# Gate and up of the second layer's experts: from float32 matmuls to three float32r products of split operands

## The chip, the cores and the metric

The kernel runs on one core of a Trainium2 chip. The metric is device time in microseconds (us), lower is better. TensorE (PE) multiplies, with its weight loads shown apart as PEld; VectorE (DVE), ScalarE (ACT) and GpSimd (POOL) work on vectors; SyncE (SP) issues most DMAs. A name with a q behind it (PEq, PEldq, DVEq) is that engine's sequencer, which reads the instruction stream, computes addresses and waits for semaphores.

## What is computed

Two layers, each cross attention and then a mixture of experts, on a sequence of 2048 tokens of width 256. The change lies in the second layer's mixture. Cut from the reference:

```python
x = hidden_states.reshape(-1, d)                 # 2048 x 256
scores = jax.nn.sigmoid(x @ W_gate_router)       # 8 experts
_, sel = jax.lax.top_k(scores + expert_bias, 2)
shared = jax.nn.silu(x @ Wg_s) * (x @ Wu_s) @ Wd_s
xr = x[tok]                                      # every token twice
h = jax.nn.silu(jnp.einsum('nd,edf->enf', xr, Wg)) * jnp.einsum('nd,edf->enf', xr, Wu)   # f = 192
out_all = jnp.einsum('enf,efd->end', h, Wd)
routed = out_all[exp, jnp.arange(exp.shape[0])] * w
out = shared.at[tok].add(routed)
```

Gate and up are the two products with Wg and Wu. Both are taken at once: 256 inputs against 2 x 192 = 384 columns.

## The kernel before, in words

The second mixture has three parts in a row, each a block that all engines leave together.

`route_and_share` computes the router, the shared branch and the place of each token in a list sorted by expert. POOL scatters the normalised tokens to that list in DRAM with 32 indirect DMAs (L1355) and at the end waits until they have landed. Meanwhile SP loads the weights of all 8 experts into SBUF (`resident["up"]` and `resident["down"]`, in the trace `keep_f_up` and `keep_f_down`), and waits for them (`resident_in`). PE, ACT and DVE compute the shared branch; its float32 products for gate and up are already made of three float32r products: a `high` part (ACT, L1410 and L1416), a `low` part, original minus `high` (DVE, L1459 and L1466), and then high x high, high x low and low x high (PE, L1389).

`run_resident_slots` works through 39 slots of 128 sorted tokens, one expert each. The order of each engine is that of the code, in a software pipeline: step s does the gate and up of slot s, the turning (transposing) of the rows of slot s + 1, the turning of the hidden values of slot s - 1 and the down product of slot s - 2. The steps 3 to 36 are a hardware loop, two steps in a pass; the others stand out straight. Within a step:

- POOL: `send(s - 5)` issues an indirect DMA of a finished slot's result (L1906), `stage_rows(s)` copies the rows of a slot (L1891).
- PE: two register loads of the expert's number from SBUF (L1934, `value_load`), which PE's sequencer turns into addresses; `go_up(s)` (L1950), `turn_rows(s + 1)` (L1941), `turn_hidden(s - 1)` (L1960), `go_down(s - 2)` (L1969). Waits stand in `wait` (L71, and L73 where it puts a nop behind the wait, `apart=True`).
- ACT: the activation of gate (L2003), then the copy of turned rows to SBUF, `x_t` (L1995).
- DVE: the product of gate and up (L2017), the copy of the turned hidden values (L2022), the copy of the result (L2026).

A float32 matmul of the program shows as two MATMUL records in the trace, so `go_up`, 2 matmuls of 384 columns, shows as 4.

`collect` then loads the results back and adds them up.

## Time and profile before

| | us |
|---|---|
| median of 3 runs (lowest, highest) | 1779.78 (1776.4, 1784.43) |
| the profiled execution, its time | 1767.28 |
| its span, first to last instruction | 1765.5 |
| PE busy | 1484.7 (84%) |
| DVE busy | 1160.5 (66%) |
| ACT busy | 856.5 (49%) |
| mean granted clock of PE | 0.914 of full speed |

The share of busy time is a mean over stages with different limits. The attention and the first layer fill the span up to about 1500 us; the change concerns what lies behind, 1522 us (start of the router) to 1743 us (start of `collect`). PE's granted clock is given as a share of 2.4 GHz: 1.00 is 2.4 GHz, 0.50 is 1.2 GHz. The PE durations of single matmuls include the time from first column to last result; how fast a row of them goes is read from the distance of their starts.

### The profile page before, as it was taken

How to read it: one execution, taken by the hardware profiler on the slowest of the kernel's cores; microseconds unless marked ns; L12 is line 12 of the kernel's file. 1: busy time of each engine (PE TensorE's matmuls, PEld its weight loads, DVE VectorE, ACT ScalarE, POOL GpSimd, SP SyncE). 2: the span in 40 equal slices, each digit the busy share in tenths (PEclk: the TensorE clock that was granted, in tenths of full speed). 3: DMA queues.
4: the chain of work that ended last, by engine and by line, in shares of the span. 5: the costliest groups of instructions: out<-in, count | busy, mean ns of one | idle time of the engine just before them, and what ended most of it. 6: DMA issues, size and time to landing. Idle time of an engine off the chain costs nothing. (4 is left out here: it accounts for less than half of the span.)

```text
span 1765.5 us, 23798 instructions
## 1 busy us (share of the span) xinstructions
PE 1484.7 (84%) x7833; PEld 870.6 (49%) x7834; DVE 1160.5 (66%) x2277; ACT 856.5 (49%) x1537; POOL 237.3 (13%) x357
## 2 busy tenths in 40 slices
PE   5769889779996999994499999999999999675883
PEld 3333333367885788883253333433443434553551
DVE  5739889464112677775399999999999973531334
ACT  3214777522212555551317777777777786231110
POOL 2000000001202333331000000000000000064443
PEclk9787999878998999997659999999999999697997
DMA  8844121120103899982533211111121100525114
GB/s 287 349 143 136 44 56 46 42 92 13 38 1 129 292 341 341 332 314 81 153 87 89 46 25 42 30 24 24 32 40 24 24 2 1 119 78 164 39 42 164
DMA packets 107534, 190.84 MB, mean 108 GB/s; under 512 B 10702, under 2 KB 80323, under 8 KB 107431
## 3 DMA queue, kind: packets, MB, share of 16 engines
q1 hardware_dynamic: 97521, 159.31, 28.7%
q0 software_dynamic: 7584, 27.93, 4.3%
q10 hardware_dynamic: 2326, 2.31, 0.4%
q8 instruction: 55, 0.90, 0.2%
q14 instruction: 48, 0.39, 0.1%
HBM read 145.20 MB, written 43.79 MB: 107 GB/s over the span
## 5 line engine op out<-in xcount | busy, mean ns | idle before, releaser
L1099 DVE TENSOR_REDUCE attend_piece_max<-attend_p_bank 128x1 f32<-128x400 f32 (+3 forms) x1280 | 669.5, 589 | 66.5 <-PE attend_p_bank L982 54.3
L1079 ACT ACTIVATE attend_probs<-attend_s_bank 128x512 f32<-128x512 f32 (+1 forms) x1053 | 549.6, 606 | 232.4 <-PE attend_s_bank L996 232.1
L982 PE MATMUL attend_p_bank<-attend_k_st,attend_q_st 62*128 62x400 f32 (+2 forms) x1280 | 416.0, 435 | 41.6 <-DMA attend_q_st<-q_rows 19.4
L996 PE MATMUL attend_s_bank<-attend_q_st,attend_k_st 64*128 64x512 f32 (+1 forms) x1053 | 390.3, 447 | 39.4 <-ACT attend_probs L1079 13.2
L996 PEld LDWEIGHTS attend_s_bank<-attend_q_st,attend_k_st 64*128 64x128 f32 (+1 forms) x1053 | 168.3, 184 | 347.3 <-ACT attend_probs L1079 326.0
L1013 PE MATMUL attend_o_bank<-attend_probs,attend_v_st 128*32 128x512 f32 (+1 forms) x2176 | 291.0, 607 | 2.2 <-ACT attend_probs L1079 2.1
L982 PEld LDWEIGHTS attend_p_bank<-attend_k_st,attend_q_st 62*128 62x128 f32 x1280 | 208.6, 195 | 89.4 <-issue 39.1
L1753 DVE TENSOR_TENSOR slots_w_low<-slots_w_up,slots_w_high 128x2048 fp32r<-128x2048 f32 x46 | 110.4, 2402 | 45.7 <-ACT slots_w_high L1749 45.7
L1540 DVE TENSOR_TENSOR share_hid<-share_b_bank,share_g_act 128x512 f32<-128x512 f32 (+1 forms) x40 | 27.6, 691 | 116.5 <-PE share_b_bank L1389 105.4
L957 POOL COPY attend_v_st<-attend_values 128x64 f32<-128x64 f32 (+1 forms) x32 | 9.2, 296 | 692.2 <-PE attend_o_bank L1013 658.3
L1749 ACT ACTIVATE slots_w_high<-slots_w_up 128x2048 fp32r<-128x2048 f32 x46 | 87.7, 1908 | 5.9 <-DMA slots_w_up<-in_L_ffn_W_dram 5.7
L1709 PE MATMUL slots_y_bank<-slots_w_dn,slots_hid_t 128*128 128x256 f32 x368 | 83.2, 379 | 1.0 <-DVE slots_hid_t L1760 1.0
L1662 POOL DMA_INDIRECT back<-slots_y_sb,slots_target x23 | 61.6, 2677 | 152.9 <-DVE slots_y_sb L1809 152.9
L2017 DVE TENSOR_TENSOR slots_hid<-slots_u_bank,slots_g_act 128x192 f32<-128x192 f32 x39 | 14.0, 358 | 101.2 <-ACT slots_g_act L2003 101.2
L1401 PE MATMUL share_y_bank<-share_w_dn,share_hid 128*128 128x256 f32 (+1 forms) x320 | 71.3, 382 | 5.9 <-DVE share_hid L1540 5.9
L1709 PEld LDWEIGHTS slots_y_bank<-slots_w_dn,slots_hid_t 128*128 128x128 f32 x368 | 69.9, 190 | 11.4 <-issue 1.2
L1013 PEld LDWEIGHTS attend_o_bank<-attend_probs,attend_v_st 128*32 128x32 f32 (+1 forms) x2176 | 43.0, 108 | 64.7 <-ACT attend_probs L1079 32.0
L1950 PE MATMUL slots_u_bank<-keep_f_up,slots_x_t 128*128 x156 | 62.0, 521 | 14.4 <-issue 11.9
L1401 PEld LDWEIGHTS share_y_bank<-share_w_dn,share_hid 128*128 128x128 f32 (+1 forms) x320 | 59.6, 190 | 17.5 <-DVE share_hid L1540 8.9
L1426 ACT ACTIVATE share_g_act<-share_a_bank 128x512 f32<-128x512 f32 (+1 forms) x40 | 23.9, 598 | 79.5 <-PE share_a_bank L1389 79.5
L1773 ACT ACTIVATE slots_g_act<-slots_a_bank 128x512 f32<-128x512 f32 x46 | 27.2, 592 | 71.3 <-PE slots_a_bank L1687 71.3
L1355 POOL DMA_INDIRECT sorted<-keep_x_x_n,keep_f_place x48 | 48.7, 1014 | 96.2 <-DVE keep_f_place L1523 82.3
(264 smaller groups left out, 1844.2 us busy)
## 6 DMA issues: line engine op xcount, KB each, us to landing
slots_w_up<-in_L_ffn_W_dram SPq DMA_DIRECT2D x46, 1024.0 KB, 7.2
slots_w_dn<-in_L_ffn_W_dram SPq DMA_DIRECT2D x23, 1024.0 KB, 5.6
prep_raw<-in_mask_BxSxS_ik_dram POOLq DMA_DIRECT2D x16, 800.5 KB, 8.4
attend_q_st<-q_rows SPq DMA_DIRECT2D x64, 128.0 KB, 3.1
sorted<-keep_zeros SPq DMA_DIRECT2D x6, 1088.0 KB, 7.8
k_rows<-prep_k_part SPq DMA_DIRECT2D x8, 800.5 KB, 6.0
attend_k_st<-k_rows SPq DMA_DIRECT2D x32, 200.1 KB, 3.6
collect_back<-back SPq DMA_DIRECT2D x12, 512.0 KB, 7.0
```

The costliest lines, as they stand in the source:

```text
L982: last = pe.matmul(bank[:, 0:even(kn)], q_st[rows, slot, t * P:(t + 1) * P].bitcast(F32R), k_st[rows, slot, k0:k0 + even(kn)].bitcast(F32R ...
L996: last = pe.matmul(out, k_st[rows, hs, kt * P:kt * P + kn].bitcast(F32R), q_st[rows, hs, q0:q0 + CH].bitcast(F32R), start=True, stop=not m ...
L1013: last = pe.matmul(o_bank[c * VW:(c + 1) * VW, :], v_st[0:kn, hs, kt, :], probs[0:kn, (kt + hs) % RING, c * CH:(c + 1) * CH], start=(kt == ...
L1079: act.activation(probs[0:kn, (kt + hs) % RING, q0:q0 + CH], score_bank(i, h, hs, kt, c)[0:kn, :], ACT.Exp).then_inc(exp_done, 1)
L1099: dve.tensor_reduce(dst, bank_of(i, n)[:, 0:kn], AX.X, ALU.max).then_inc(entry_done, 1)
L1355: pool.indirect_dma_start(scratch["sorted"][l][:, :], bass.IndirectOffsetOnAxis(ap=place[:, k, t:t + 1], axis=0), x_n[:, t], None).then_in ...
L1401: last = pe.matmul(y_bank[n % 2][:, :], hid[:, c % 2, f, t * P:(t + 1) * P], w_dn[:, f], start=(f == 0), stop=(f == FT - 1))
L1662: pool.indirect_dma_start(scratch["back"][l][:, :], bass.IndirectOffsetOnAxis(ap=target[:, s:s + 1], axis=0), y_sb[:, s % 2], None)\
L1709: last = pe.matmul(y_bank[:, 0:D], hid_t[:, slot, f], w_dn[:, slot, f], start=(f == 0), stop=(f == FT - 1))
L1749: act.activation(w_high[:, half].bitcast(F32R), loaded(slot, half), ACT.Copy).then_inc(w_rounded, 1)
L1753: dve.tensor_tensor(w_low[:, half].bitcast(F32R), loaded(slot, half), w_high[:, half], ALU.subtract)\
L1950: last = pe.matmul(u_bank[k][:, 0:2 * F], x_t[:, k, b], resident["up"][:, e, b].rearrange("p a n f -> p (a n f)"), start=(b == 0), stop=(b ...
```

## The change

At the end of `route_and_share`, behind the last work of ACT and DVE there, 8 operations of ACT round each expert's gate and up weights to float32r into a new tile `high`, and 8 of DVE replace the weights in `up` by weights minus `high`. In `run_resident_slots` the turned rows are split in the same way: ACT writes `x_high`, DVE `x_low`. `go_up` is six float32r matmuls of 384 columns in place of two float32 matmuls, and in a step `turn_rows(s + 1)` now stands ahead of `go_up(s)`; on ACT the rounding of the rows stands ahead of the activation.

```diff
@@ route_and_share, scalar @@
+            if resident:
+                act.wait_ge(resident_in, 16 * 3 * E)
+                for e in range(E):
+                    act.activation(resident["high"][:, e].bitcast(F32R), resident["up"][:, e], ACT.Copy)\
+                        .then_inc(expert_high, 1)
@@ route_and_share, vector @@
+            if resident:
+                for e in range(E):
+                    dve.wait_ge(expert_high, e + 1)
+                    dve.tensor_tensor(resident["up"][:, e].bitcast(F32R), resident["up"][:, e], resident["high"][:, e],
+                                      ALU.subtract).then_inc(expert_low, 1)
@@ run_resident_slots, tensor @@
             def go_up(s, k, e):
-                wait(pe, x_copied, s + 1, apart=True)
+                wait(pe, x_split, s + 1, apart=True)
                 if again(s):
                     wait(pe, hid_ready, s - 1, apart=True)
-                for b in range(DB):
-                    last = pe.matmul(u_bank[k][:, 0:2 * F], x_t[:, k, b],
-                                     resident["up"][:, e, b].rearrange("p a n f -> p (a n f)"), start=(b == 0),
-                                     stop=(b == DB - 1))
+                products = [(x, resident[w], b) for b in range(DB)
+                            for x, w in ((x_high, "high"), (x_high, "up"), (x_low, "high"))]
+                for p, (x, w, b) in enumerate(products):
+                    last = pe.matmul(u_bank[k][:, 0:2 * F], x[:, k, b].bitcast(F32R),
+                                     w[:, e, b].rearrange("p a n f -> p (a n f)").bitcast(F32R), start=(p == 0),
+                                     stop=(p == len(products) - 1))
                 last.then_inc(up_ready, 1)
...
             def body(s, k):
...
+                if is_slot(s + 1):
+                    turn_rows(s + 1, 1 - k)
                 if is_slot(s):
                     go_up(s, k, up)
-                if is_slot(s + 1):
-                    turn_rows(s + 1, 1 - k)
@@ run_resident_slots, scalar @@
-            def copy_rows(s, k):
+            def round_rows(s, k):
...
-                act.activation(x_t[:, k], x_bank[k][:, 0:DB * P].rearrange("p (b q) -> p b q", b=DB), ACT.Copy)\
-                    .then_inc(x_copied, 1)
+                act.activation(x_high[:, k].bitcast(F32R), turned_rows(k), ACT.Copy).then_inc(x_rounded, 1)
@@ run_resident_slots, vector @@
+            def split_rows(s, k):
+                wait(dve, x_rounded, s + 1)
...
+                dve.tensor_tensor(x_low[:, k].bitcast(F32R), turned_rows(k), x_high[:, k], ALU.subtract)\
+                    .then_inc(x_split, 1)
@@ flamingo_kernel @@
+                                "high": keep.sb("high", [P, E, DB, 2, m.F], F32),
```

The first place where instructions change is PE's stream in the first step of the loop's pass. In these rows TENSOR_LOAD, ISA and REGISTER_ALU are work of the sequencer (loading the expert's number, computing addresses and the counts to wait for); L1950 is `go_up`, L1941 `turn_rows`, L1960 `turn_hidden`, L1969 `go_down`. Before:

```order
L1934 TENSOR_LOAD keep_f_slot_expert
L1934 ISA x2
L71 REGISTER_ALU x2
L1950 ISA
L1950 MATMUL slots_u_bank<-keep_f_up,slots_x_t 128x384
L1950 ISA
L1950 MATMUL slots_u_bank<-keep_f_up,slots_x_t 128x384
L71 REGISTER_ALU
L1941 MATMUL slots_x_bank<-keep_ident,slots_stage 128x128 x2
L1960 MATMUL slots_h_bank<-keep_ident,slots_hid 96x128 x2
```

In the changed kernel the same stretch reads as follows; its lines are numbered otherwise, L1944 for L1934, L1951 for L1941, L1962 for L1950 and L1972 for L1960:

```order
L71 REGISTER_ALU
L1951 MATMUL slots_x_bank<-keep_ident,slots_stage 128x128 x2
L71 REGISTER_ALU x2
L1962 ISA
L1962 MATMUL slots_u_bank<-keep_f_high,slots_x_high 128x384
L1962 REGISTER_ALU
L1962 MATMUL slots_u_bank<-keep_f_up,slots_x_high 128x384
L1962 MATMUL slots_u_bank<-keep_f_high,slots_x_low 128x384
L1962 ISA
L1962 MATMUL slots_u_bank<-keep_f_high,slots_x_high 128x384
L1962 REGISTER_ALU
L1962 MATMUL slots_u_bank<-keep_f_up,slots_x_high 128x384
```

One more product of the same kind follows, and then the turning of the hidden values. The turning of the rows moved ahead of gate and up, and within gate and up stand two sequencer instructions more than before, a REGISTER_ALU for each half.

The second place is the end of the shared branch on DVE, where L1540 is the last product of the shared branch. Before:

```order
L1466 TENSOR_TENSOR share_x_low<-keep_x_x_nt,share_x_high 128x1024
L1540 TENSOR_TENSOR share_hid<-share_b_bank,share_g_act 96x512 x2
L1273 UNCONDITIONAL_BRANCH
L2010 UNCONDITIONAL_BRANCH
L2017 TENSOR_TENSOR slots_hid<-slots_u_bank,slots_g_act 128x192 x2
```

In the changed kernel (L1545 stands for L1540, L1471 for L1466, L2030 is the split of the rows and L2040 stands for L2017):

```order
L1471 TENSOR_TENSOR share_x_low<-keep_x_x_nt,share_x_high 128x1024
L1545 TENSOR_TENSOR share_hid<-share_b_bank,share_g_act 96x512 x2
L1554 TENSOR_TENSOR keep_f_up<-keep_f_up,keep_f_high 128x768 x8
L1273 UNCONDITIONAL_BRANCH
L2024 UNCONDITIONAL_BRANCH
L2030 TENSOR_TENSOR slots_x_low<-slots_x_bank,slots_x_high 128x256 x2
L2040 TENSOR_TENSOR slots_hid<-slots_u_bank,slots_g_act 128x192
```

Eight subtractions of 128x768 with both inputs in SBUF have come in ahead of the end of the block, and in the slots a subtraction of 128x256 for each slot.

## Rows read from the trace of the kernel before

**Rows 1.** Stretch, length; PE, PEld, DVE, ACT, POOL busy; PE clock, DMA share, GB/s

```profile
1618.00:1720.00 102.00, 90.18 (x380) 57.70 (x380) 34.77 (x94) 18.79 (x63) 47.09 (x68) 1.00 0.13 46
```

**Rows 2.** PE in order of time, one pass of the loop: start, length

```profile
1663.50 1.55 PE L1950 MATMUL slots_u_bank<-keep_f_up,slots_x_t 128*128 x4 [0.61 <-issue]
1664.88 0.38 PE L1941 MATMUL slots_x_bank<-keep_ident,slots_stage 128*128 128x128 f32 x2
...
1665.32 1.03 PE L1969 MATMUL slots_y_bank<-keep_f_down,slots_hid_t 96*128 x4
1666.44 1.55 PE L1950 MATMUL slots_u_bank<-keep_f_up,slots_x_t 128*128 x4
...
1670.04 1.55 PE L1950 MATMUL slots_u_bank<-keep_f_up,slots_x_t 128*128 x4 [0.74 <-issue]
```

**Rows 3.** Who waited for whom, 1618 to 1720: total us, times, longest

```profile
PE slots_u_bank L1950 <- issue: 10.8, 15, 0.8
```

**Rows 4.** PE's sequencer, 1663.34 to 1664.36: ns min/median/max, first and last start

```profile
L1950 PEldq FUSED_REGOPS  x2: 46/46/46, 1663.4 to 1663.5; - x2
L71 PEldq ALU_OP  x2: 32/32/32, 1663.6 to 1664.1; - x2
L71 PEldq EVENT_SEMAPHORE  x2: 51/51/51, 1663.7 to 1663.9; - x2
L73 PEldq EVENT_SEMAPHORE  x2: 51/51/51, 1664.0 to 1664.2; - x2
L1969 PEldq FUSED_REGOPS  x1: 46/46/46, 1664.3 to 1664.3; - x1
```

**Rows 5.** The same view of the register loads, 1618 to 1720

```profile
L1934 PEldq TENSOR_LOAD <-keep_f_slot_expert x63: 295/306/545, 1619.2 to 1719.8; - x63
```

**Rows 6.** PE in order of time, the first layer's experts in float32r

```profile
704.13 0.39 PE L1687 MATMUL slots_a_bank<-slots_w_low,slots_x_high 128*128 128x512 f32 x1
...
706.45 0.40 PE L1687 MATMUL slots_b_bank<-slots_w_high,slots_x_low 128*128 128x512 f32 x1
```

**Rows 7.** Split operations by line: ns min/median/max, first and last start

```profile
L1466 DVE TENSOR_TENSOR share_x_low<-keep_x_x_nt,share_x_high x8: 1209/1218/1221, 402.1 to 1568.4; 128x1024 fp32r<-128x1024 f32 x8
L1459 DVE TENSOR_TENSOR share_w_low<-share_w_up,share_w_high x2: 553/556/558, 1529.3 to 1529.8; 128x384 fp32r<-128x384 f32 x2
L1410 ACT ACTIVATE share_x_high<-keep_x_x_nt x8: 1040/1050/1057, 384.8 to 1566.9; 128x1024 fp32r<-128x1024 f32 x8
L1739 DVE TENSOR_TENSOR slots_x_low<-slots_x_bank,slots_x_high x23: 412/416/425, 556.9 to 788.6; 128x256 fp32r<-128x256 f32 x23
```

**Rows 8.** POOL, in order of time, beside the shared branch

```profile
1557.59 0.96 POOL L1355 DMA_INDIRECT sorted<-keep_x_x_n,keep_f_place  x1 [0.30 <-issue]
1568.23 2.27 POOL L1355 DMA_INDIRECT sorted<-keep_x_x_n,keep_f_place  x1 [0.30 <-issue]
```

**Rows 9.** DVE, in order of time, the same stretch

```profile
1557.69 0.69 DVE L1540 TENSOR_TENSOR share_hid<-share_b_bank,share_g_act 96x512 f32<-96x512 f32 x1 [0.16 <-PE share_b_bank L1389]
1558.30 1.21 DVE L1466 TENSOR_TENSOR share_x_low<-keep_x_x_nt,share_x_high 128x1024 fp32r<-128x1024 f32 x1
...
1568.45 1.21 DVE L1466 TENSOR_TENSOR share_x_low<-keep_x_x_nt,share_x_high 128x1024 fp32r<-128x1024 f32 x1
```

**Rows 10.** All engines in order of time, from the shared branch to the first slots

```profile
1582.53 0.47 ACT L1431 ACTIVATE keep_f_acc<-share_y_bank,keep_gates 128x256 f32<-128x256 f32 x1 [0.39 <-PE share_y_bank L1401]
...
1596.88 0.96 POOL L1355 DMA_INDIRECT sorted<-keep_x_x_n,keep_f_place  x1 [0.30 <-issue]
1602.48 0.37 SPq L1881 DMA_DIRECT2D slots_rows<-sorted  x1
...
1607.63 0.69 PE L1941 MATMUL slots_x_bank<-keep_ident,slots_stage 128*128 128x128 f32 x2 [25.14 <-POOL slots_stage L1891]
...
1608.88 2.92 PE L1950 MATMUL slots_u_bank<-keep_f_up,slots_x_t 128*128 x4 [0.56 <-ACT slots_x_t L1995]
...
1611.59 0.64 PE L1941 MATMUL slots_x_bank<-keep_ident,slots_stage 128*128 128x128 f32 x2
```

More of the change, by code:

```diff
@@ L1316, in route_and_share @@
         y_ready, y_copied = sc.sem("y_ready"), sc.sem("y_copied")
-        resident_in = sc.sem("resident_in")
+        resident_in, expert_high, expert_low = sc.sem("resident_in"), sc.sem("expert_high"), sc.sem("expert_low")
         scattered, numbered = const["scattered"][l], sc.sem("numbered")
@@ L1845, in run_resident_slots @@
         stage = sc.sb("stage", [P, 2, D], F32)
-        x_t = sc.sb("x_t", [P, 2, DB, P], F32)
+        x_high, x_low = (sc.sb(f"x_{n}", [P, 2, DB, P], F32) for n in ("high", "low"))
         g_act = sc.sb("g_act", [P, 2, F], F32)
@@ L1852, in run_resident_slots @@
         head_in, rest_in, staged = sc.sem("head_in"), sc.sem("rest_in"), sc.sem("staged")
-        x_turned, x_copied = sc.sem("x_turned"), sc.sem("x_copied")
+        x_turned, x_rounded, x_split = sc.sem("x_turned"), sc.sem("x_rounded"), sc.sem("x_split")
         up_ready, activated, hid_ready = sc.sem("up_ready"), sc.sem("activated"), sc.sem("hid_ready")
@@ L1938, in turn_rows @@
                 if again(s):
-                    wait(pe, x_copied, s - 1)
+                    wait(pe, x_split, s - 1)
                 for b in range(DB):
@@ L1987, in _, with turned_rows @@
             steps(pe, body)
+        def turned_rows(k):
+            return x_bank[k][:, 0:DB * P].rearrange("p (b q) -> p b q", b=DB)
         @block.scalar
         def _(act):
-            def copy_rows(s, k):
+            def round_rows(s, k):
                 wait(act, x_turned, s + 1)
@@ L1994, in copy_rows @@
                     wait(act, up_ready, s - 1)
-                act.activation(x_t[:, k], x_bank[k][:, 0:DB * P].rearrange("p (b q) -> p b q", b=DB), ACT.Copy)\
-                    .then_inc(x_copied, 1)
+                act.activation(x_high[:, k].bitcast(F32R), turned_rows(k), ACT.Copy).then_inc(x_rounded, 1)
             def body(s, k):
+                if is_slot(s + 1):
+                    round_rows(s + 1, 1 - k)
                 if is_slot(s):
@@ L2003, in body @@
                     act.activation(g_act[:, k], u_bank[k][:, 0:F], m.func).then_inc(activated, 1)
-                if is_slot(s + 1):
-                    copy_rows(s + 1, 1 - k)
-            copy_rows(0, 0)
+            round_rows(0, 0)
             steps(act, body)
@@ L2011, in _ @@
         def _(dve):
+            def split_rows(s, k):
+                wait(dve, x_rounded, s + 1)
+                if again(s):
+                    wait(dve, up_ready, s - 1)
+                dve.tensor_tensor(x_low[:, k].bitcast(F32R), turned_rows(k), x_high[:, k], ALU.subtract)\
+                    .then_inc(x_split, 1)
             def body(s, k):
+                if is_slot(s + 1):
+                    split_rows(s + 1, 1 - k)
                 if is_slot(s):
@@ L2027, in body @@
                         .then_inc(y_copied, 1)
+            split_rows(0, 0)
             steps(dve, body)
```

## The prediction, before the changed kernel had run

> **What bounds the kernel now.** I read the busy time by stretch first, then the order of time on PE in the loop of the slots, then the waits, then PE's sequencer, and last the passage from the shared branch to the slots.
>
> In the steady stretch of the slots PE is busy 90.18 of 102 us at the full clock of 2.4 GHz [rows 1]. That looks like a stage bound by the array, and then cheaper matmuls pay. The order of time says otherwise. Gate and up start at 1663.50, 1666.44 and 1670.04 [rows 2]: one pass of two slots takes 6.54 us, 3.27 us a slot. The busy figure counts each matmul up to its last result; what the array needs is the distance of starts. Gate and up take 1664.88 - 1663.50 = 1.38 us until the turning of the rows starts, the two turnings 1665.32 - 1664.88 = 0.44, and the down product 1666.44 - 1665.32 = 1.12 at most. That is 2.94 us in the short step, and in the long one the array stands idle ahead of gate and up, by 0.61 and 0.74 us, and the releaser is "issue" [rows 2]: no semaphore, no other engine. Over the stretch this idle time comes to 10.8 us in 15 steps [rows 3]. Nobody made PE wait; its own sequencer came late.
>
> So I read the sequencer. Between the first address computation of gate and up (1663.4) and that of the down product (1664.3) stand 8 sequencer instructions in 0.9 us: 2 of 46 ns, 2 of 32 and 4 of 51 [rows 4], 0.36 us of their own time and so about 0.07 us of gap behind each. Every one lasts its usual 51 ns or less, so none of them is a wait that blocked. All 8 are issued while the array is still in the first three quarters of gate and up. To these comes, in each step, the pair of register loads with a median of 306 ns, up to 545 [rows 5], with address work behind each. The step is the length of this list; the array follows behind it.
>
> The second bound lies ahead of the slots. ACT ends the shared branch at 1582.53 + 0.47 = 1583.0; POOL goes on issuing scatters until 1596.88 + 0.96; the block ends when they have landed and SP can start at 1602.48; PE starts at 1607.63 after 25 us of nothing [rows 10]. POOL's issue of the scatters is the path here, and ACT and DVE are idle beside it.
>
> **The change part by part.** *The products.* Two float32 matmuls of 384 columns give way to six float32r ones. Float32r of 512 columns starts every (706.45 - 704.13)/10 = 0.232 us [rows 6]; scaled to 384 columns that is 0.174, six are 1.04 us. Against 1.38 us the array saves 0.34 us a slot at most, 39 x 0.34 = 13 us if the array bound the step. Since the sequencer bounds it, I count this as zero, and look at what the sequencer gets: two REGISTER_ALU more a slot, at 32 ns and 0.07 of gap, 0.10 us each by [rows 4]. That is 0.20 us a slot, 39 x 0.20 = 7.8 us more. The four added matmuls with their weight loads have no row of their own on the sequencer; the gaps of [rows 4] that hold them are not visibly longer, so I take nothing, with 0.1 us a slot (3.9 us) as the upper end. Below: the long second register load after the branch (545 instead of about 306 ns) may fall elsewhere in the changed pass; it is worth 0.24 us in some 17 passes, 4 us either way. The step goes from 3.27 to 3.47 us.
>
> *The order of turning and gate and up.* The list of waits is the same, only permuted, and none of them blocks now. The rows of slot s + 1 are needed 1.38 us earlier in the step, but the step is 0.2 us longer. POOL waits for the result of a slot rather than the reverse, except in the last few steps, where its additions (L1926) already pace it. Zero.
>
> *The split of the rows.* ACT does what it did. DVE gets a subtraction of 0.42 us [rows 7] a slot, one input in PSUM; DVE is busy 34.77 of 102 us [rows 1], so 32 x 0.42 = 13 us more have room. The result is needed one step later. Hidden, apart from slot 0, where it adds 0.42 us and a semaphore, about 0.5 us.
>
> *The start of the slots.* Gate and up of slot 0 run at 1.2 GHz and take 1611.59 - 1608.88 = 2.7 us [rows 10]; float32r at that clock takes 6 x 384 / 1.2 GHz = 1.92 us, and slot 1's rows are turned ahead of them instead of behind. I take 1.5 us off, with 0.5 added by the split: -1.0 us.
>
> *The split of the weights.* 8 operations of 128x768 on ACT, 8 on DVE, from 1583.0 on. On DVE 384 columns take 0.556 us and 1024 take 1.218 [rows 7], so 768 take 0.95; consecutive ones overlap a little, I take 0.88 apart, 7.0 us in all. ACT is no slower (1.05 against 1.22 us for 1024 columns, [rows 7]), so DVE runs from about 1584 to 1591 without a gap. By DVE's and ACT's idle time this is free. But it lies beside POOL's scatters. One indirect DMA takes 0.96 us; the one at 1568.23 took 2.27 [rows 8], and in it fell a subtraction with both inputs in SBUF, 1.21 us from 1568.45 on. The product at 1557.69, with one input in PSUM, fell into the DMA at 1557.59, which took its 0.96 [rows 8, 9]. So a DVE operation that reads two SBUF tensors stops POOL's issue for its whole length (1.31 for 1.21 us). The 8 new ones are of that kind. Back to back they stop POOL for 7.0 us, and every later scatter, the landing and the first slot come 7.0 us later. If POOL gets one issue in at each seam, it loses about 2 of the issues that stand 1.27 us apart: 2.6 us. The row that I have is a full stop, so 7.0.
>
> The Trainium skill has this as a rule (SBUF — State Buffer, section "SBUF: two separate sides"): VectorE and GpSimd share a port pair as an exclusive lock, a VectorE operation with two SBUF inputs is one that takes it, and the other side blocks fully. Of this the trace agrees, with 2.27 against 0.96 us. The page also says that whichever starts first holds the pair to its end. The trace shows it otherwise for POOL's DMAs: the one at 1568.23 was under way for 0.22 us when the subtraction began, and was stopped. By the page a DMA issue once begun would run through and a subtraction would wait for it, which is the 2.6 us; by the rows it is the 7.0.
>
> **The sum.** +7.8 (sequencer) + 7.0 (POOL stopped) - 1.0 (start) = +13.8 us. The profiled execution goes from 1767.28 to 1781.1; the median of the runs stands 12.5 us above that execution, so 1779.78 + 13.8 = 1793.6 us.
>
> **Rivals.**
> 1. The array bounds the slots after all: the busy share of 88% speaks for it [rows 1], the idle time by "issue" against it. The slots gain up to 13 us, 10 as a middle; with the stop of POOL and the start: -10 + 7.0 - 1.0 = -4, 1776 us.
> 2. The same, and POOL isn't held up: -10 - 1 = -11, 1769 us. It needs two readings of mine to be wrong.
> 3. POOL slips in between the subtractions (2.6 us), the sequencer as forecast: 7.8 + 2.6 - 1.0 = +9.4, 1789 us. For it speaks that POOL only needs the port in part of an issue: the subtraction at 1558.30 began 0.71 us into one that still took its 0.96 [rows 8, 9].
> 4. PE's clock falls, since the array has gaps of 1 us and more in a step. The array's 2.94 - 0.34 = 2.6 us a slot would double to 5.2 in place of 3.27, 39 x 1.9 = 75 us, with the other two terms +81: 1861 us. Against it: the clock stayed at 1.00 with idle times of 0.6 to 0.7 us in every other step [rows 1, 2].
> 5. The change doesn't reach the fast rate: float32r of 384 columns on resident weights running like float32. Then six products take three times 1.38 us, the step becomes 2.94 + 2.76 = 5.7 us, 39 x 2.4 = 95 us, with the other two terms +101: 1881 us. The first layer's 0.232 us for 512 columns speaks against it.
>
> **How the numbers follow.** My forecast 60%, rival 3 15%, rival 1 12%, rival 2 5%, rival 4 3%, rival 5 2%, other 3%. The forecast's own range is 7.8 (-4, +4) + 7.0 (-4.4, +0.5) - 1.0 (1.5 either way): 1785 to 1800. The range that should hold the time 8 in 10 reaches down towards rival 1 and up by the spread of runs, which is 8 us here: 1780 to 1803. A measurement of this kernel tells 0.5% (8.9 us) from no change. Slower by more: nearly all of the forecast, half of rival 3, the rivals 4 and 5 and a part of the rest, 0.74. Within it: half of rival 3 and rival 1 with the low edge of the forecast, 0.20. Faster: 0.06.
>
> **What would show it.** In the scatters (L1355): one or more issues of POOL between 1584 and 1591 far over 0.96 us, and the last issue near 1604 instead of 1596.9. The first turning in the slots near 1614.6 instead of 1607.6. The distance of gate and up in the loop: 6.9 us for two slots instead of 6.54, with the idle time by "issue" on PE grown from 10.8 to some 25 us. Six products within 1.1 us. If the distance is below 6.5 us, the sequencer wasn't the bound and the main step fails; if POOL's issues keep 0.96 us, the second step fails.

## The result, and the profile after

The changed kernel took 1796.71 us (median of 7 runs), the kernel before 1783.22 (7 runs beside them): ratio 1.0071, 95% interval [1.0054, 1.0088], so slower by 9.6 to 15.7 us. It was forecast at 1793.6 us, +13.8. Run once more in the experiments, in a later session in which the kernel before took 1768.33 us, it stood at 1.0049 [1.0034, 1.0065] against it, +8.7 us (6.0 to 11.5); the two intervals overlap. From session to session the unchanged kernel took 1768 to 1783 us, so only ratios within one session are compared. The sign and the main step came out; the second term did not.

The first profile of the changed kernel (span 1795.0 us) holds something that belongs to that execution alone. ACT at the end of the shared branch, start, length, and in brackets the idle time before and its releaser:

```profile
1582.61 0.47 ACT L1431 ACTIVATE keep_f_acc<-share_y_bank,keep_gates 128x256 f32<-128x256 f32 x1 [2.40 <-PE share_y_bank L1401]
1586.89 0.47 ACT L1431 ACTIVATE keep_f_acc<-share_y_bank,keep_gates 128x256 f32<-128x256 f32 x1 [3.81 <-remote]
...
1600.33 0.59 ACT L1426 ACTIVATE share_g_act<-share_a_bank 96x512 f32<-96x512 f32 x1 [8.68 <-remote]
1609.53 0.59 ACT L1426 ACTIVATE share_g_act<-share_a_bank 96x512 f32<-96x512 f32 x1 [8.61 <-remote]
```

And PE in the same stretch: its last gate and up products of the shared branch, and then the down products, which waited 19 us for DVE.

```profile
1590.84 0.62 PE L1389 MATMUL share_b_bank<-share_x_low,share_w_high 128*96 128x512 f32 x2
1610.90 5.57 PE L1401 MATMUL share_y_bank<-share_w_dn,share_hid 96*128 96x256 f32 x16 [19.44 <-DVE share_hid L1545]
```

By the profile PE had its products done by 1591.5, but ACT took the step that waits for the first of them only at 1600.33, and the second at 1609.53; DVE, whose first product was done by 1588.7, went on at 1609.51. The ends of matmuls are modelled in the profile, from their starts. It therefore can't tell signals that came late from products that were finished late; I call them late signals below. The split of the weights then fell behind the last scatter and was exposed, so that 66.3 us lay between the first scatter and the first turning of the slots. (Of the 29.5 us by which this execution's span exceeds that of the profile before, 8.8 lie ahead of the first scatter, where the kernels are the same.) None of the twelve profiles that follow shows it again. So I read the changed kernel in its second profile (span 1775.9 us, execution 1777.6). POOL's scatters there, and DVE's eight subtractions:

```profile
1584.05 1.72 POOL L1355 DMA_INDIRECT sorted<-keep_x_x_n,keep_f_place  x1 [0.30 <-issue]
1586.08 1.44 POOL L1355 DMA_INDIRECT sorted<-keep_x_x_n,keep_f_place  x1 [0.30 <-issue]
1587.82 1.43 POOL L1355 DMA_INDIRECT sorted<-keep_x_x_n,keep_f_place  x1 [0.30 <-issue]
1589.26 0.94 POOL L1351 COPY keep_x_x_n<-keep_index 128x4 f32<-128x4 f32 x1
1590.48 1.40 POOL L1355 DMA_INDIRECT sorted<-keep_x_x_n,keep_f_place  x1 [0.28 <-POOL keep_x_x_n L1351]
1592.18 0.96 POOL L1355 DMA_INDIRECT sorted<-keep_x_x_n,keep_f_place  x1 [0.30 <-issue]
```

```profile
1583.99 7.04 DVE L1554 TENSOR_TENSOR keep_f_up<-keep_f_up,keep_f_high 128x768 fp32r<-128x768 f32 x8 [5.08 <-ACT keep_f_high L1436]
```

Four issues take 1.40 to 1.72 instead of 0.96 us [rows 8], and a copy 0.94 instead of 0.20: 2.9 us in all. The end of the scatters and the way to the slots, for [rows 10]:

```profile
1599.96 0.96 POOL L1355 DMA_INDIRECT sorted<-keep_x_x_n,keep_f_place  x1 [0.30 <-issue]
1605.56 0.37 SPq L1891 DMA_DIRECT2D slots_rows<-sorted  x1
...
1610.64 1.37 PE L1951 MATMUL slots_x_bank<-keep_ident,slots_stage 128*128 128x128 f32 x4 [27.93 <-POOL slots_stage L1901]
```

There is a second wait, a few slots later, that I had not forecast. POOL copies the rows of slot 5 only when all the later rows have landed. Before, and then in the changed kernel, with PE's turning of these rows:

```profile
1620.68 0.39 POOL L1891 COPY slots_stage<-slots_rows 128x256 f32<-128x256 f32 x1 [0.34 <-DMA slots_rows<-sorted]
```

```profile
1624.98 0.39 POOL L1901 COPY slots_stage<-slots_rows 128x256 f32<-128x256 f32 x1 [3.17 <-DMA slots_rows<-sorted]
1625.43 0.44 PE L1951 MATMUL slots_x_bank<-keep_ident,slots_stage 128*128 128x128 f32 x2 [2.51 <-POOL slots_stage L1901]
```

In the kernel before, gate and up of slot 4 (at 1621.00) stood ahead of this turning (at 1622.39), and PE did not wait. Now the turning stands first, and PE waits 2.51 us: from slot 3 to slot 4 it takes 5.22 us where it took 2.97. The last of the loads landed 13.0 us after the first turning before, 14.3 us after it now; why it is later I haven't found. Behind this wait the granted clock was 0.50 from 1626.7 to 1629.8, and 1.00 again from 1630 to 1722.

In the loop, PE in order of time (for [rows 2]):

```profile
1671.03 0.44 PE L1962 MATMUL slots_u_bank<-keep_f_high,slots_x_high 128*128 x1
1671.30 0.34 PE L1962 MATMUL slots_u_bank<-keep_f_up,slots_x_high 128*128 x1
...
1672.00 0.34 PE L1962 MATMUL slots_u_bank<-keep_f_high,slots_x_low 128*128 x1
1672.17 0.38 PE L1972 MATMUL slots_h_bank<-keep_ident,slots_hid 128*96 128x128 f32 x2
1672.39 1.03 PE L1981 MATMUL slots_y_bank<-keep_f_down,slots_hid_t 96*128 x4
1673.82 0.41 PE L1951 MATMUL slots_x_bank<-keep_ident,slots_stage 128*128 128x128 f32 x2 [0.40 <-issue]
1674.15 0.44 PE L1962 MATMUL slots_u_bank<-keep_f_high,slots_x_high 128*128 x1
...
1677.29 0.41 PE L1951 MATMUL slots_x_bank<-keep_ident,slots_stage 128*128 128x128 f32 x2 [0.74 <-issue]
1677.80 0.44 PE L1962 MATMUL slots_u_bank<-keep_f_high,slots_x_high 128*128 x1
```

The six products start 0.17 to 0.27 us apart and are through in 1.14 us, where two float32 ones took 1.38. Yet this pass takes 1677.80 - 1671.03 = 6.77 us, and the idle time by "issue" now stands ahead of the turning of the rows, which opens the step. The stretch of 102 us from 1620 on (columns as in [rows 1]), and who waited there (for [rows 3]):

```profile
1620.00:1722.00 102.00, 81.66 (x406) 62.16 (x406) 44.07 (x116) 20.78 (x58) 41.59 (x62) 0.98 0.14 47
```

```profile
PE slots_x_bank L1951 <- issue: 16.3, 26, 1.0
...
PE slots_u_bank L1962 <- issue: 0.5, 3, 0.2
```

PE is less busy than before, 81.66 against 90.18 us, and the stage is longer. Set side by side, the two profiled executions (1767.28 and 1777.6, +10.3) divide so:

| from, to | before | after | |
|---|---|---|---|
| start to first scatter | 1555.03 | 1555.25 | +0.2 |
| first scatter to first turning of the slots | 52.60 | 55.40 | +2.8 |
| first turning to the end of the last send | 129.97 | 137.82 | +7.85 |
| rest | 27.9 | 27.4 | -0.5 |

### The profile page after: what moved, and what is told of

It is laid out like the page before. It is cut to its first block and busy times, and to the rows that moved or that the text cites. A ratio compares the mean times of both kernels' runs of the same rounds, so it can differ in the third digit from the quotient of the medians.

```text
span 1795.0 us, 24141 instructions
## 1 busy us (share of the span) xinstructions
PE 1489.8 (83%) x7911; PEld 886.5 (49%) x7912; DVE 1183.8 (66%) x2324; ACT 866.8 (48%) x1545; POOL 238.6 (13%) x357
## 5 line engine op out<-in xcount | busy, mean ns | idle before, releaser
L1099 DVE TENSOR_REDUCE attend_piece_max<-attend_p_bank 128x1 f32<-128x400 f32 (+3 forms) x1280 | 669.5, 590 | 66.3 <-PE attend_p_bank L982 54.1
L1545 DVE TENSOR_TENSOR share_hid<-share_b_bank,share_g_act 128x512 f32<-128x512 f32 (+1 forms) x40 | 27.5, 691 | 145.4 <-PE share_b_bank L1389 88.7
L1719 PEld LDWEIGHTS slots_y_bank<-slots_w_dn,slots_hid_t 128*128 128x128 f32 x368 | 69.8, 190 | 11.5 <-issue 1.2
L1697 PE MATMUL slots_a_bank<-slots_w_high,slots_x_high 128*128 128x512 f32 x92 | 43.5, 473 | 14.9 <-DVE slots_w_low L1763 11.9
L1431 ACT ACTIVATE keep_f_acc<-share_y_bank,keep_gates 128x256 f32<-128x256 f32 x32 | 15.2, 474 | 82.1 <-PE share_y_bank L1401 71.5
```

Source lines behind the costliest of these rows:

```text
L1099: dve.tensor_reduce(dst, bank_of(i, n)[:, 0:kn], AX.X, ALU.max).then_inc(entry_done, 1)
L1697: last = pe.matmul(bank[half][:, 0:HW], x[:, slot, b].bitcast(F32R), w[:, half, which, b].bitcast(F32R), start=(p == 0), stop=(p == len(pr ...
L1719: last = pe.matmul(y_bank[:, 0:D], hid_t[:, slot, f], w_dn[:, slot, f], start=(f == 0), stop=(f == FT - 1))
```

## The experiments

All were timed in five rounds against the kernel before, on the same chip. The "pass" is the mean distance of gate and up over two slots, from slot 4 to slot 34 (15 passes); the "passage" goes from the first scatter to the first turning, the "slots" from there to the end of the last send. The "later pass" leaves out the wait for the rows of slot 5 and the low clock behind it: it is the mean from slot 6 to slot 34 (14 passes). The "instructions" are those that PE's sequencer executes in one pass, counted in the trace. The last five columns are one profiled execution each.

| kernel | ratio | 95% interval | pass | later pass | instructions | passage | slots |
|---|---|---|---|---|---|---|---|
| before | 1 | | 6.49 | 6.50 | 43 | 52.6 | 130.0 |
| changed, again | 1.0049 | 1.0034, 1.0065 | 6.92 | 6.93 | 47 | 55.4 | 137.8 |
| split only | 1.0009 | 0.9997, 1.0020 | 6.48 | 6.48 | 43 | 55.5 | 129.8 |
| products only | 0.9984 | 0.9973, 0.9996 | 6.37 | 6.35 | 43 | 52.6 | 129.9 |
| half the array's work | 0.9997 | 0.9986, 1.0009 | 6.62 | 6.42 | 43 | 52.5 | 129.9 |
| two tiles | 1.0003 | 0.9994, 1.0012 | 6.43 | 6.44 | 43 | 52.7 | 129.2 |
| one tile | 1.0058 | 1.0046, 1.0071 | 6.99 | 6.99 | 47 | 55.3 | 138.9 |
| four addresses | 1.0027 | 1.0017, 1.0037 | 6.85 | 6.83 | 47 | 52.5 | 137.4 |
| late split | 1.0033 | 1.0016, 1.0049 | 6.93 | 6.93 | 47 | 52.5 | 137.9 |
| written out, before | 0.9897 | 0.9883, 0.9911 | 5.19 | 5.19 | 22 | 52.6 | 112.3 |
| written out, changed | 0.9886 | 0.9872, 0.9900 | 5.10 | 4.95 | 26 | 54.8 | 111.8 |
| written out, late split | 0.9870 | 0.9855, 0.9884 | 5.06 | 4.95 | 26 | 52.6 | 111.0 |
| written out, direct rows | 0.9828 | 0.9812, 0.9844 | 4.71 | 4.71 | 24 | 52.0 | 100.5 |

The looped kernels fall into two groups. With 43 sequencer instructions a pass the later pass takes 6.35 to 6.50 us, whether gate and up is four records of float32 matmuls, half their columns or six float32r products; with 47 it takes 6.83 to 6.99. Between the means of the groups, 6.44 and 6.92, lie 0.48 us for four instructions, 0.12 us each; the kernel before and the changed one give 0.11, other pairs 0.08 to 0.16.

**The changed kernel again**, unaltered.

> The changed kernel once more, unaltered, to see which parts of its profile return. My two steps: the first turning of the slots to the last send takes 137 us again (129.0 before), and the first scatter to the first turning 7 us longer than before (about 60 against 52.6), with the vector engine's eight weight subtractions running from about 1590 while the scatters are still being issued, which then wait. The profile seen already showed another picture in the second part: the scalar and the vector engine got their signals from the tensor engine up to 19 us late in the shared branch, and the weight split began only after all scatters had been issued, 66.3 us from the first scatter to the first turning. If that belongs to the change, it returns here at about the same place and size; if it was a chance of one execution, it is gone and the part takes 59 to 61 us. Time against the kernel before: 1.0075.

Measured: 1.0049; the slots term returned (137.8 against 137.9 us in the first profile), the late signals did not. The passage grew by 2.8 us, neither 7 nor 13.7. The wait for the rows of slot 5 was in the first profile too (5.40 us from slot 3 to slot 4).

**Split only.** The kernel before, with these lines at the end of the shared branch (and the tile `high`):

```diff
+ act.activation(resident["high"][:, e].bitcast(F32R), resident["up"][:, e], ACT.Copy)   # x 8
+ dve.tensor_tensor(resident["high"][:, e].bitcast(F32R), resident["up"][:, e], resident["high"][:, e], ALU.subtract)
```

> The kernel before with only the split of the resident weights at the end of the shared branch (eight scalar roundings, eight vector subtractions of 128x768, the difference going to the new tile); the slots multiply in float32 as before. My theory of the scatters held by the subtractions: +7.0 us. Rival, a scatter's issue slips in between two subtractions: +2.6 us. Rival, the split is exposed whole behind the shared branch: +8.5 to +14 us. If the split is hidden: 0. The distance of the slots' steps stays as before in all of them.

Measured: +1.6 us (-0.5 to +3.5), passage +2.9. The first two of the four long issues:

```profile
1583.07 1.71 POOL L1355 DMA_INDIRECT sorted<-keep_x_x_n,keep_f_place  x1 [0.30 <-issue]
1585.08 1.43 POOL L1355 DMA_INDIRECT sorted<-keep_x_x_n,keep_f_place  x1 [0.30 <-issue]
```

My 7.0 falls; the rival's 2.6, where POOL slips in between two subtractions, holds.

**Products only.** The changed kernel, less the subtraction, with the rounded weights in place of their remainder:

```diff
- for x, w in ((x_high, "high"), (x_high, "up"), (x_low, "high"))]
+ for x, w in ((x_high, "high"), (x_high, "high"), (x_low, "high"))]
```

> The changed kernel without the vector engine's eight subtractions of the weights; the second product of each slot reads the rounded weights instead of their remainder, so the low part of the weights is left out of the result. The scalar engine's eight roundings stay. Three float32r products a block of rows, as many as in the change. My theory that the tensor engine's instruction queue bounds a step of the slots: +6.8 us (7.8 for the two added register operations a slot, less 1.0 at the start). Rival, the array bounds it: -11 us. If the changed kernel's loss lies in the split alone: 0.

Measured: -2.8 us (-4.8 to -0.7). Neither theory had this; in the slots the shorter passes and the quicker start are paid back by the wait for the rows of slot 5, which this kernel has as well. But my edit had taken away more than I thought: the second product now read the same weights as the first, so that a slot had two addresses of weights and not four. PE's sequencer in one pass, the address computations of gate and up (count, ns min/median/max), in this kernel:

```profile
L1957 PEldq FUSED_REGOPS  x4: 46/48/51, 1663.5 to 1669.8; - x4
```

in the kernel before:

```profile
L1950 PEldq FUSED_REGOPS  x4: 46/48/51, 1663.5 to 1669.9; - x4
```

and in the changed kernel:

```profile
L1962 PEldq ALU_OP  x4: 32/32/32, 1671.0 to 1674.4; - x4
...
L1962 PEldq FUSED_REGOPS  x4: 46/48/51, 1671.2 to 1677.7; - x4
```

Six float32r products with four address computations a pass run like two float32 ones with four, the same products with eight take 0.55 us a pass more. The subtractions that this kernel also lacks don't touch the pass (split only: 6.48 us with them).

**Half the array's work.** The kernel before with 192 columns, one product for both:

```diff
- last = pe.matmul(u_bank[k][:, 0:2 * F], x_t[:, k, b], resident["up"][:, e, b]...
+ last = pe.matmul(u_bank[k][:, 0:F], x_t[:, k, b], resident["up"][:, e, b, 0:1]...
```

> The kernel before with each float32 gate and up matmul narrowed from 384 to 192 columns (the gate's half; up's half is left out and the vector engine multiplies with the gate's columns instead). As many tensor engine instructions as before; the array saves about 0.64 us a slot. If the tensor engine's instruction queue bounds the step: 0 us, within 2, and 6.5 us a loop pass of two slots as before. Rival, the array bounds it: -25 us, 5.2 us a pass.

Measured: -0.5 us (-2.5 to +1.6). The array's work in gate and up is cut in half, and the whole of it appears as idle time on PE:

```profile
1666.50 0.91 PE L1950 MATMUL slots_u_bank<-keep_f_up,slots_x_t 128*128 x4 [1.16 <-issue]
...
1669.65 0.91 PE L1950 MATMUL slots_u_bank<-keep_f_up,slots_x_t 128*128 x4 [0.94 <-issue]
...
1673.17 0.42 PE L1950 MATMUL slots_u_bank<-keep_f_up,slots_x_t 128*128 x1 [1.30 <-issue]
```

```profile
PE slots_u_bank L1950 <- issue: 28.3, 28, 1.4
```

28.3 us in the stretch from 1618 to 1720, where the kernel before has 10.8 [rows 3]. That the array bounds the slots is refuted. The mean pass of 6.62 us contains a wait of 1.5 us for the rows of slot 5, which this kernel reaches sooner; from slot 6 on it takes 6.42 us, 0.08 less than before, where 1.3 less would have come if the array were the bound.

**Two tiles, one tile.** Two kernels that were meant to add and to remove the two register operations, through the number of tiles (in the first the weights are also loaded by smaller DMAs, one for each block of rows):

```diff
- resident = {"up": keep.sb("up", [P, E, DB, 2, m.F], F32),                       # before
+ resident = {"up0": keep.sb("up0", [P, E, 2, m.F], F32), "up1": keep.sb("up1", [P, E, 2, m.F], F32),
```

```diff
- (x_high, "high"), (x_high, "up"), (x_low, "high")      # changed: two tiles
+ (x_high, 1), (x_high, 0), (x_low, 1)                   # parts = keep.sb("up", [P, E, 2, DB, 2, m.F], F32)
```

> The kernel before with the resident gate and up weights in two tiles, one per block of rows, instead of one: the second float32 product of a slot then needs an address register of its own, two register operations more a slot on the tensor engine's queue, as in the change; matmuls, their number and all else as before. If these operations alone are what the slots lost in the change: +7.5 us, and 6.93 us a loop pass instead of 6.5. Rival, the loss is the float32r products' or their order's: 0.

> The changed kernel with the rounded weights and their remainder in one tile, so that one address register serves all six products: the two register operations a slot that the change added are gone, the arithmetic is the change's. If they are what the slots lost: 7.5 us below the changed kernel, +2 us (ratio 1.001) against before, the loop pass back at 6.4 to 6.5 us; what is left is the 2.9 us by which the weight split delays the scatters. Rival, the products themselves cost it (a product with the low part's weights): as the changed kernel, +8.7 us.

Measured: +0.5 us (-1.1 to +2.1) and +10.3 us (8.1 to 12.6). Both expectations missed. The sequencer's rows say why: in the one, two of the four address computations of a pass turned from a fused operation into a plain one; in the other, four plain ones turned into fused ones. Their number stayed, 4 and 8 a pass. In the kernel with one tile:

```profile
L1961 PEldq FUSED_REGOPS  x8: 37/48/65, 1671.8 to 1678.7; - x8
```

So the number of address computations follows the number of distinct addresses of gate and up weights, whatever the tiles, and the pass follows it: 6.44 us with 4, 6.99 with 8. Blocks b = 0 and b = 1 of one tile need one each already.

**Four addresses.** So the count of addresses alone was changed, in the kernel before:

```diff
- last = pe.matmul(u_bank[k][:, 0:2 * F], x_t[:, k, b], resident["up"][:, e, b]...           # 2 a slot
+ last = pe.matmul(u_bank[k][:, n * F:(n + 1) * F], x_t[:, k, b], resident["up"][:, e, b, n:n + 1]...   # 4 a slot
```

> The kernel before with each float32 gate and up matmul of 384 columns cut into two of 192, gate's and up's: the same columns in the array, but four weight addresses a slot, each with a register operation of its own on the tensor engine's queue, as the change has, instead of two. If each address costs 0.1 us of the queue: two more a slot, +7.8 us, the loop pass at 6.9 us. Rival, only the float32r products are dear: 0, pass 6.5 us. (Two tiles instead of one was no test of it: there are two addresses a slot either way.)

```profile
1668.84 1.56 PE L1951 MATMUL slots_u_bank<-keep_f_up,slots_x_t 128*128 x8 [0.29 <-issue]
...
1672.48 1.56 PE L1951 MATMUL slots_u_bank<-keep_f_up,slots_x_t 128*128 x8 [0.78 <-issue]
...
1675.67 0.42 PE L1951 MATMUL slots_u_bank<-keep_f_up,slots_x_t 128*128 x1 [0.33 <-issue]
```

Measured: pass 6.85 and slots +7.4 us in the profile, without any float32r; in time +4.8 us (3.0 to 6.6). The sign is clear and the pass is the expected one, but the timed size is some 2 us below the profile's, and I can't say where these are. This kernel also issues four matmuls a slot for two, so the matmuls' own issue is not fully parted from their addresses here; products only, with six matmuls and two addresses a slot and no loss, is what parts them.

**The steps written out.** PE's 41 steps as straight code, with the expert's register kept for its down product:

```diff
-     down = expert_of(s - 2) if is_slot(s - 2) else None
+     down = experts.pop(s - 2, None)
- steps(pe, body)
+ for s in range(NS + 2):
+     body(s, s % 2)
```

> The kernel before with the tensor engine's 41 steps of the slots written out instead of looped, and each slot's expert register kept for its down product two steps later: constant waits, one register load a slot instead of two, no branch. Matmuls and their order as before. If the instruction queue bounds the step: the 0.6 and 0.74 us idle ahead of the gate and up products of a pass go, and the pass falls to at most 5.9 us, -13 to -26 us. Rival, the array or another engine bounds it: 0, or a gain below 3 us.

The branch that goes with the loop, in a pass of the kernel before:

```profile
L1865 PEldq COMPARE_BRANCH  x1: 208/208/208, 1667.5 to 1667.5; - x1
```

> The changed kernel with the tensor engine's 41 steps of the slots written out and the expert's register kept for two steps, as in the written-out kernel before, whose tensor engine then had no idle time: 5.19 us a pass and 18 us faster than before. With the queue out of the way the products should now give what the array saves: 1.29 us for two float32 matmuls against six times 0.175 us, 0.24 us a slot, -9 us against the written-out kernel before; with +2.9 for the weight split and -1 at the start, ratio to before 0.986 (1742 us on that chip). Rival, the queue or the chain of turning, rounding and splitting takes over: no faster than the written-out kernel before, 0.990 to 0.992.

Before, written out, two slots:

```profile
1653.31 1.46 PE L1950 MATMUL slots_u_bank<-keep_f_up,slots_x_t 128*128 x4
1654.60 0.38 PE L1941 MATMUL slots_x_bank<-keep_ident,slots_stage 128*128 128x128 f32 x2
...
1655.90 1.46 PE L1950 MATMUL slots_u_bank<-keep_f_up,slots_x_t 128*128 x4
...
1658.50 0.49 PE L1950 MATMUL slots_u_bank<-keep_f_up,slots_x_t 128*128 x1
```

From slot 2 to slot 36 the profile shows no idle time on PE: 5.19 us a pass, and -18.2 us (-20.7 to -15.7) in time. Nothing of the array's work was changed. With that, the change no longer loses, 0.9886 against 0.9897, but of the 9 us that I expected from it only some 2 came (the two intervals overlap, and they are from two chips). The rival that something else takes over is the right one, though the chain that does is one of POOL's. Who waited from 1640 to 1700 in the changed kernel written out:

```profile
PEld slots_x_bank L1951 <- POOL slots_stage L1901: 6.4, 23, 0.4
```

The turning of the rows now waits for POOL's copy into the stage, which stands behind the send of an earlier slot on POOL's queue. (PEld is the weight load; PE itself shows no gap there, as its modelled ends cover it.) The steps are 2.57 and 2.37 us by turns, 4.95 us a pass, so half of the 0.48 us a pass that the array saves arrives. The wait for the rows of slot 5 is also there and costs more than in the loop:

```profile
1629.67 0.69 PE L1951 MATMUL slots_x_bank<-keep_ident,slots_stage 128*128 128x128 f32 x2 [3.02 <-POOL slots_stage L1901]
```

The granted clock was 0.50 from 1630 to 1634.5 behind it. From slot 3 to slot 6 this kernel takes 13.0 us, the written-out kernel before 7.8.

**The subtractions moved** behind POOL's last scatter issue (signalled by a small memset on POOL): four at the end of the shared branch, four at the start of the slots.

```diff
+     pool.memset(mark[:, :], 0.0).then_inc(issued, 1)
+     dve.wait_ge(issued, 1)
-     for e in range(E):
+     for e in range(E // 2):
```

> The changed kernel with the vector engine's eight weight subtractions moved behind the last scatter's issue: four at the end of the shared branch once GpSimd has issued its last scatter, four at the start of the slots. If their meeting with the scatters' issues costs 2.9 us: 2.9 us below the changed kernel, +5.8 us against before (1.0033), scatters' issues back at 0.96 us and 42.8 us from first to last. Rival, the split only comes to lie ahead of the slots instead: as the changed kernel, +8.7 us (1.005).

> Both: the changed kernel with the tensor engine's steps written out and the weight subtractions moved behind the last scatter's issue. If the two effects add: 2.9 us below the written-out changed kernel, ratio to before 0.984, and the fastest so far. Rival: no different from the written-out changed kernel.

```profile
1608.09 3.56 DVE L1558 TENSOR_TENSOR keep_f_up<-keep_f_up,keep_f_high 128x768 fp32r<-128x768 f32 x4 [19.33 <-issue]
1612.64 3.56 DVE L2058 TENSOR_TENSOR keep_f_up<-keep_f_up,keep_f_high 128x768 fp32r<-128x768 f32 x4 [0.98 <-PEq L1273]
1618.76 0.42 DVE L2035 TENSOR_TENSOR slots_x_low<-slots_x_bank,slots_x_high 128x256 fp32r<-128x256 f32 x1 [2.56 <-ACT slots_x_high L2015]
```

The passage is back at 52.5 and 52.6 us, as expected, and the last subtraction ends 2.6 us before the first split of rows. In the looped kernels the gain in time is not told apart from zero (1.0033 against 1.0049, in two sessions). The two written-out kernels ran in the same rounds on one chip, four executions each: 1755.79 to 1756.42 us without the edit, 1752.97 to 1754.72 with it. They don't overlap, and the medians lie 2.7 us apart, close to the 2.9 expected.

**Rows turned directly.** With constant steps PE can read the rows where they land:

```diff
- pool.tensor_copy(stage[:, s % 2], rows[:, s, 0:D]).then_inc(staged, 1)
- last = pe.transpose(x_bank[k][:, b * P:(b + 1) * P], stage[:, k, b * P:(b + 1) * P],
+ last = pe.transpose(x_bank[k][:, b * P:(b + 1) * P], rows[:, s, b * P:(b + 1) * P],
```

> The last kernel (the change, tensor engine's steps written out, subtractions behind the last scatter) with the slots' rows turned straight from the tile in which they land: as the steps are constants now, GpSimd's copies into the stage are not needed, and each of the three later loads of rows is waited for by itself. In the written-out changed kernel the turnings still waited for these copies, which stand behind the sends on GpSimd's queue (3.0 us once, and about 0.2 us a slot: steps of 2.55 us against about 2.33 us without a wait). If that chain bounds it: the pass falls from 5.06 to 4.65 us, 8 us, and the first wait's 3 us go, ratio to before 0.981 (0.979 to 0.984). Rival, the array or the vector engine bounds it: as the kernel without this edit, 0.987.

```profile
1647.85 0.39 PE L1948 MATMUL slots_x_bank<-keep_ident,slots_rows 128*128 128x128 f32 x2
1647.99 0.42 PE L1959 MATMUL slots_u_bank<-keep_f_high,slots_x_high 128*128 x1
...
1650.21 0.38 PE L1948 MATMUL slots_x_bank<-keep_ident,slots_rows 128*128 128x128 f32 x2
1650.35 0.42 PE L1959 MATMUL slots_u_bank<-keep_f_high,slots_x_high 128*128 x1
```

PE is busy without a gap, 4.71 us a pass, and the wait for the rows of slot 5 is gone too. The kernel takes 1738.52 us against 1769.48 of the kernel before on that chip, ratio 0.9828 [0.9812, 0.9844], 30 us faster (28 to 33): the fastest of all. Against the written-out kernel with the late split the slots are 10.5 us shorter. Only 3.4 us of that are the steadily shorter passes (4.95 to 4.71 us); 5.9 us come from slots 3 to 6, where the wait and the low clock behind it were, and the remainder from the end. The same edit was not tried on the kernel before with float32 products. There, written out, PE waited for POOL's copies only twice, 1.0 us each near the end, so by this trace it has little to gain from it; that is argued and not run.

## Why the prediction was right, and where not

**The queue bounds the slots: right.** Half the array's work in gate and up taken away changed nothing, a lighter queue with the same work took 18 us off. The forecast of 3.47 us a step came out as 3.46 (6.92 a pass). The terms, by the profile of the kernel before and the second one of the changed kernel:

| term | forecast | measured |
|---|---|---|
| sequencer, in the loop | +7.8 | +6.5 (15 passes of 0.43 us) |
| order of turning and gate and up | 0 | +2.25 (slot 3 to slot 4) |
| start of the slots | -1.0 | -0.5 |
| POOL stopped | +7.0 | +2.8 |
| everything else | 0 | -0.7 |
| sum | +13.8 | +10.3 |

The start is the first three distances, 9.15 to 8.17 us, less 0.46 later at the first product. The stage of the slots grew by 7.85 us. That looks like the 7.8 of the sequencer and is so by chance: it holds 6.5 of the sequencer, since 9 of the 39 slots lie in stretches that other waits set, and the 2.25 of a wait that I had not counted. My reason for the two operations, that a second tile needs a register of its own, was too narrow: it is each further address.

**The order of turning and gate and up: a term put at zero.** I had written that the rows "are needed 1.38 us earlier in the step" and counted zero, since none of the waits blocked in the steady passes. For slot 5 the rows come late, and with the turning ahead of gate and up PE waits 2.51 us for them. The order can account for the 1.14 us of a gate and up that would otherwise run during the wait; the quicker start and the load that landed 1.3 us later add to it. No run puts the old order back into the changed kernel, so the parts are read from the traces and not shown singly.

**Idle time by "issue" on PE.** I had said from 10.8 to some 25 us; it is 16.8 by name, while the time in which PE isn't busy went from 11.8 to 20.3 of 102 us. The array's saving is 0.24 us a slot, within my "0.34 us a slot at most": the written-out kernels without idle time show 5.19 against 4.71 us a pass.

**POOL stopped by the subtractions: the step that failed.** "The row that I have is a full stop, so 7.0" measured 2.8 to 2.9, and 2.3 in the written-out kernel. The eight subtractions start 0.87 us apart, at 1583.99, 1584.86, 1585.73, 1586.60, 1587.47, 1588.34, 1589.21 and 1590.08, each 0.95 long. An issue that begins at 1584.05 would wait 0.81 us for the next of these seams, and took 0.76 longer; those at 1586.08 and 1587.82 would wait 0.52 each, and took 0.48 and 0.47 longer; the copy at 1589.26 0.82 and 0.74. The issue at 1590.48 met the last subtraction, would wait 0.55 for its end and took 0.44 longer. So POOL waits out the subtraction under way and then runs, beside the next one. My row [rows 8] had a single subtraction in it, with nothing behind; it could not tell a stop of one operation from a stop of a row of them, and I carried the one over to the other. Rival 3 (2.6 us, 15%) was the right one for this term, and its 1789 us, +9.4, is nearer to the repeat (+8.7) than my +13.8; the first comparison (13.5 us between the medians) is nearer to mine, but its profile had the 2.8 us of POOL in no place and the late signals instead. That the forecast met that median is in part chance.

The Trainium skill (SBUF — State Buffer, section "SBUF: two separate sides") says that of a VectorE operation with two SBUF inputs and a GpSimd one that reads SBUF, whichever starts first holds the port pair to its end. For the beginning of the four long issues here this agrees: the subtraction was first each time, and POOL got on at its end. It doesn't say who is next at a seam; here it was POOL, at each of the four seams, and the next subtraction was not late for it. That the two then ran side by side (the issue of 1584.05 to 1585.77, the subtraction from 1584.86 to 1585.81) is not what a pair held for the whole instruction would give. The stop in [rows 8], where POOL's DMA was first, still speaks against the rule.

**The clock, the rate of float32r:** granted clock 1.00 from 1630 to 1722, products 0.17 us apart. Rivals 4 and 5 fall. The 0.98 of the whole stretch is the 3.1 us at half clock behind the wait for slot 5's rows, and there the looped kernel lost nothing visible by it (6.83 us for the pass from slot 4 to slot 6, against 6.93 later); the written-out one took 7.26 against 4.95. Rivals 1 and 2 fall with half the array's work.

**Open:** what made ACT and DVE go on up to 21 us after PE's products in the first profile, and whether it was also in the other six runs of that comparison; their intervals overlap, so the difference between 1.0071 and 1.0049 may be no more than noise. Of the written-out steps, the dropped branch, the dropped register load and the constant waits were not parted.

## What to carry over

Where a loop with register addresses leaves PE idle by "issue", count what its sequencer executes in a step (register operations and waits, each about 0.1 us with its gap, the branch nearly 0.3, a register load 0.35 and more; by [rows 4], [rows 5] and the row of the branch) before making the matmuls cheaper: a cheaper product that needs more distinct addresses costs time. Write the steps out first and keep loaded registers; then the array is the bound and the cheaper product pays, once the next chain is cut as well. Before an operation is moved ahead of another, look at the first passes too: an input that is late only once waits only there, and a steady stretch doesn't show it. A cost read from one meeting of two engines holds for one meeting: for a row of operations look for what happens at the seams.

## What the hardware showed that I had not expected

- A new address for a matmul's operand under a register index cost about 0.11 us of PE's queue: four more a pass, +0.36 us (four addresses) to +0.50 us (one tile) against the kernel before, no matter whether they lay in the same tile or in another.
- Six float32r matmuls of 384 columns cost the queue nothing measurable more than two float32 ones (6.37 against 6.49 us a pass, with the same four address computations); in the trace the two float32 ones are four records [rows 2], the six float32r ones six.
- A POOL indirect DMA issue and a VectorE subtraction with two SBUF inputs: held 0.44 to 0.76 us, to the end of the subtraction under way; then POOL ran beside the next one.
- In one profiled execution of fourteen, ACT and DVE went on up to 21 us after the modelled ends of the PE products that they waited for, while POOL issued indirect DMAs at its usual 0.96 us. The cause is open.
